# Attended values as plain float32 products of 64 columns, two heads side by side, without a split of the probabilities

## What is computed

```python
q = rms_norm(h @ wq_a, q_a_norm_w) @ wq_b            # 16 heads, 64 latent + 64 rotary columns
compressed_kv, k_pe = split(h @ wkv_a)                # 64 + 64, the same for all heads
attn = einsum('bhqd,bhkd->bhqk', query, key) * SCALE  # 512 x 512 per sequence and head
attn = softmax(attn, axis=-1)
out = einsum('bhqk,bhkd->bhqd', attn, value)          # "attended values"
return out.reshape(b, s, NH * 64) @ wo
```

## Time and profile before

| | |
|---|---|
| median of 3 runs | 1203.41 us (1202.18 to 1204.48) |
| profiled execution: its own time | 1212.62 us |
| its span, first to last instruction | 1210.8 us |
| mean granted TensorE clock | 0.956 |
| busy share of the span | PE 86%, weight loads 72%, DVE 68%, ACT 51%, POOL 41% |
| instructions | PE 6200, DVE 1750, ACT 1340, POOL 464 |

### The profile page before, as it was taken

The page is one execution under the profiler, slowest core; times in us unless marked ns, Lnnn a source line. Parts: engine busy times, 40 slices in busy tenths (PEclk is TensorE's granted clock), DMA queues, the critical chain, the costliest instruction groups (busy, mean ns, idle before and its releaser), DMA issues.

```text
span 1210.8 us, 24733 instructions
## 1 busy us (share of the span) xinstructions
PE 1046.0 (86%) x6200; PEld 865.9 (72%) x6201; DVE 822.8 (68%) x1750; ACT 617.0 (51%) x1340; POOL 501.7 (41%) x464
## 2 busy tenths in 40 slices
PE   4559999997446999999999999999989739999995
PEld 4537777786434788888888888888778627777784
DVE  6354665544674999999999999999834455566542
ACT  2232433422113888888888888888810123343321
POOL 2532233233233455555555555555412532233332
PEclk9999999999676999999999999999999859999998
DMA  9733544422200011111111000101464464454230
GB/s 241 244 128 67 138 100 100 104 47 27 70 0 1 10 36 36 35 35 35 35 35 34 27 31 31 35 35 35 140 217 144 131 209 96 106 141 102 48 54 11
DMA packets 71562, 95.41 MB, mean 79 GB/s; under 512 B 9600, under 2 KB 48640, under 8 KB 71296
## 3 DMA queue, kind: packets, MB, share of 16 engines
q1 hardware_dynamic: 57216, 78.04, 20.8%
q0 software_dynamic: 14304, 16.87, 7.9%
HBM read 64.37 MB, written 34.43 MB: 82 GB/s over the span
## 4 chain that ended last, share of the span: by engine, by line
PE 73%; issue 10%; DVE 6%; POOL 3%; ACT 3%; DMA 1%; another core or an unknown queue 1%; DVEq 1%; ACTq 0%; SPq 0%; POOLq 0%
PE bank L1537 9%; PE bank L1553 7%; PE bank L1356 6%; PE bank L1354 5%; PE bank L1527 5%; PE bank L1358 5%; PE bank L1554 5%; PE bank L1528 5%; PE bank L1529 5%; PE bank L1339 3%; PE bank L1366 3%; PE bank L1368 3%; PE bank L1367 3%; PE bank L1516 2%; PE bank L1517 2%
## 5 line engine op out<-in xcount | busy, mean ns | idle before, releaser
L811 ACT ACTIVATE shared<-bank,small 128x512 f32<-128x512 f32 x256 | 176.1, 688 | 58.6 <-DVE small L1186 56.3
L1186 DVE TENSOR_REDUCE small<-bank 128x1 f32<-128x512 f32 x256 | 175.3, 685 | 38.8 <-PE bank L1529 28.5
L1216 DVE TENSOR_TENSOR split_rows_and_inner<-bank,shared_split 128x512 fp32r<-128x512 f32 x256 | 174.7, 683 | 7.3 <-ACT shared_split L820 5.9
L762 ACT CAST split_rows_and_inner<-bank 128x512 fp32r<-128x512 f32 x78 | 45.9, 588 | 257.0 <-PE bank L1339 232.0
L1537 PE MATMUL bank<-constants,shared 128*128 128x128 f32 x1024 | 155.7, 274 | 0.9 <-ACT shared L811 0.9
L1553 PE MATMUL bank<-shared_split 128*128 128x256 f32 x512 | 144.1, 304 | 5.5 <-DVE shared L1210 2.3
L820 ACT CAST shared_split<-bank 128x512 fp32r<-128x512 f32 x256 | 147.6, 577 | 1.0 <-PE bank L1537 1.0
L1356 PE MATMUL bank<-expert_weights_low,split_rows_and_inner 128*128 x312 | 144.0, 462 | 0.0
L1358 PE MATMUL bank<-expert_weights_high,split_rows_and_inner 128*128 x312 | 143.0, 458 | 0.0
L1553 PEld LDWEIGHTS bank<-shared_split 128*128 128x128 f32 x512 | 96.2, 188 | 56.8 <-issue 27.9
L1554 PE MATMUL bank<-split_rows_and_inner,shared_split 128*128 128x256 f32 x512 | 132.7, 282 | 0.0
(11 more groups left out here) (191 smaller groups left out, 2480.6 us busy)
## 6 DMA issues: line engine op xcount, KB each, us to landing
expert_weights<-L_ffn_w_kernel SPq DMA_DIRECT2D x32, 512.0 KB
shared<-rows_by_expert SPq DMA_DIRECT2D x78, 129.0 KB, 2.4
expert_weights<-L_ffn_wo_kernel SPq DMA_DIRECT2D x16, 512.0 KB
shared<-inverse_sums SPq DMA_DIRECT2D x64, 128.0 KB, 2.8
attended_transposed<-shared SPq DMA_DIRECT2D x32, 256.0 KB, 2.8
expert_weights<-attended_transposed SPq DMA_DIRECT2D x2, 2048.0 KB, 10.1
shared<-attended_transposed SPq DMA_DIRECT2D x2, 2048.0 KB
rows_by_expert<-empty_rows SPq DMA_DIRECT2D x23, 129.0 KB
```

The lines of the kernel that those rows point to most:

```text
L811: nc.scalar.activation(prob[k % 2], bank[k % 4][:, :], ACT.Exp, bias=negmax[:, k % 8:k % 8 + 1], accum_out=psum[par][:, k % 8:k % 8 + 1]). ...
L1186: V.tensor_reduce(negmax[:, k % 8:k % 8 + 1], bank[k % 4][:, :], AX.X, ALU.max, negate=True).then_inc(max_ready, 1)
L1216: V.tensor_tensor(pTl[k // 2 % 2][:, :, at], bank[4 + k % 2][:, :].rearrange("p (c n) -> p c n", c=GT), pTh[k // 2 % 2][:, :, at].bitcast( ...
```

## The change

The two heads of a pair are worked on in turn: tile k is head k % 2, queries k // 2. The transposed probabilities are copied once, as plain float32, tiles 0, 1, 4, 7 by ACT and 2, 3, 5, 6 by DVE, into four buffers (half, head). `attend` takes one chunk c of one half for both heads: two float32 products with 64 columns of values, one into partitions 0 to 63 of bank 6, one into 64 to 127. A half has 256 queries of both heads and eight such products; half 0 is computed at k = 5, 6 and 7 (two chunks at 7), half 1 at k = 0 to 3 of the next pair; k = 4 has none. The lower parts of probabilities and values, `add_lower` and ACT's `take_output` are gone. DVE takes the whole of bank 6 out once a pair, at k = 4. The split query weights have two buffers, and their second fill no longer waits for a query product. The diff, cut (left out: unchanged lines around the edits, names of semaphores, the query products' buffer index, waits in SP's list, the setup's value copies, the removed `add_lower` and ACT's `take_output`):

```diff
@@ -52,8 +52,10 @@
-F32_SHARED = 13 * S + P
-F32R_SHARED = 4 * GT * 3 * HD + 8 * S + 2 * GT * 2 * P + 2 * 3 * P
+F32_SHARED = 11 * S + P
+PT_WORDS = 2 * 2 * GT * 2 * P
+F32R_SHARED = 8 * S + PT_WORDS + (B + 2) * GT * HD + 4 * 3 * P
+BY_ACT, BY_DVE = (0, 1, 4, 7), (2, 3, 5, 6)
...
@@ -266,19 +267,19 @@
-        raw, rawl, inv, att = ([area((5 + 2 * n + k) * S, [S]) for k in range(2)] for n in range(4))
-        invT = area(13 * S, [P], 8)
+        raw, inv, att = ([area((5 + 2 * n + k) * S, [S]) for k in range(2)] for n in range(3))
+        invT = area(11 * S, [P], 8)
         o = 0
         qh, ql = ([[split_area(split, o + (4 * k + 2 * par + hh) * S, [S]) for hh in range(2)] for par in range(2)]
                   for k in range(2))
         o += 8 * S
-        pTh = [split_area(split, o + k * GT * 2 * P, [GT, 2 * P]) for k in range(2)]
-        pTl = [split_area(parts, k * GT * 2 * P, [GT, 2 * P]) for k in range(2)]
-        o += 2 * GT * 2 * P
-        vcur = [split_area(split, o + par * 2 * GT * 3 * HD, [2, GT, 3 * HD]) for par in range(2)]
-        o += 4 * GT * 3 * HD
-        wch, wcl = (split_area(split, o + k * 3 * P, [3, P]) for k in range(2))
+        pT = [[area(F32_SHARED + o + (half * 2 + hh) * GT * 2 * P, [GT, 2 * P]) for hh in range(2)] for half in range(2)]
+        o += PT_WORDS
+        values = area(F32_SHARED + o, [B, GT, HD])
+        o += B * GT * HD
+        vcur = [area(F32_SHARED + o + par * GT * HD, [GT, HD]) for par in range(2)]
+        o += 2 * GT * HD
+        wch, wcl = ([split_area(split, o + (2 * k + par) * 3 * P, [3, P]) for par in range(2)] for k in range(2))
...
@@ -360,6 +360,17 @@
+        def tile(k):
+            return k % 2, k // 2
+        def wait_pT(eng, p, k):
+            if k in BY_ACT:
+                eng.wait_ge(pT_by_act, p * len(BY_ACT) + BY_ACT.index(k) + 1)
+            else:
+                eng.wait_ge(pT_by_dve, p * len(BY_DVE) + BY_DVE.index(k) + 1)
...
@@ -558,25 +569,22 @@
-            def load_weights(p, used):
+            def load_weights(p, par, used):
                 a = p % PAIRS if isinstance(p, int) else pool.snap(p % PAIRS)
                 src = wpair[:, bass.ds(a, 1), :, :].rearrange("p a s n -> p (a s) n")
                 if used is not None:
                     pool.wait_ge(qz_psum, used)
-                nc.gpsimd.tensor_copy(wch, src).then_inc(wc_high, 1)
+                nc.gpsimd.tensor_copy(wch[par], src).then_inc(wc_high, 1)
                 pool.wait_ge(wc_high, p + 1)
                 pool.sem_inc(wc_low_due, 1)
-                nc.gpsimd.tensor_tensor(wcl, src, wch.bitcast(F32), ALU.subtract).then_inc(wcur_ready, 1)
+                nc.gpsimd.tensor_tensor(wcl[par], src, wch[par].bitcast(F32), ALU.subtract).then_inc(wcur_ready, 1)
             def load_values(p, par, used):
                 if used is not None:
                     pool.wait_ge(o_psum, used)
-                high, low = (src[:, bass.ds(p // PAIRS, 1), :, :] for src in (vh, vl))
-                nc.gpsimd.tensor_copy(vcur[par][:, :, :, HD:2 * HD], high.to_broadcast([P, 2, GT, HD]))
-                nc.gpsimd.tensor_copy(vcur[par][:, 0, :, :].rearrange("p t (n c) -> p t n c", n=3)[:, :, 0:3:2, :],
-                                      low.rearrange("p a t n -> p t a n").to_broadcast([P, GT, 2, HD])).then_inc(vcur_ready, 1)
+                nc.gpsimd.tensor_copy(vcur[par].unsqueeze(1), values[:, bass.ds(p // PAIRS, 1), :, :]).then_inc(vcur_ready, 1)
...
@@ -649,13 +643,10 @@
-                    load_weights(p + 2, p + 2)
+                    load_weights(p + 2, par, p + 1)
                 if not last:
                     rope_lower(p + 1, 1 - par)
-                if not among(p, 0):
-                    add_lower(p - 1, 1 - par)
-                if not last:
-                    load_values(p + 1, 1 - par, None if among(p, 0) else p * 4)
+                    load_values(p + 1, 1 - par, None if among(p, 0) else p * 2)
...
@@ -805,20 +795,23 @@
+                hh, qt = tile(k % 8)
                 act.wait_ge(max_ready, s + 1)
                 if not first:
                     act.wait_ge(pT_psum, s - 1)
                 nc.scalar.activation(prob[k % 2], bank[k % 4][:, :], ACT.Exp,
                                      bias=negmax[:, k % 8:k % 8 + 1],
-                                     accum_out=psum[par][:, k % 8:k % 8 + 1]).then_inc(exp_ready, 1)
-            def high_probs(p, k, first):
+                                     accum_out=psum[par][:, hh * GT + qt:hh * GT + qt + 1]).then_inc(exp_ready, 1)
+            def copy_pT(p, k, first):
+                hh, qt = tile(k)
+                half = qt // 2
                 act.wait_ge(pT_psum, p * 8 + k + 1)
-                if k % 2 == 0 and not (first and k < 4):
-                    act.wait_ge(o_psum, p * 4 + k // 2 - 1)
-                nc.scalar.copy(pTh[k // 2 % 2][:, :, (k % 2) * P:(k % 2 + 1) * P],
-                               bank[4 + k % 2][:, :].rearrange("p (c n) -> p c n", c=GT)).then_inc(pT_high, 1)
+                if k in (BY_ACT[0], BY_ACT[2]) and not first:
+                    act.wait_ge(o_psum, p * 2 + half - 1)
+                nc.scalar.copy(pT[half][hh][:, :, (qt % 2) * P:(qt % 2 + 1) * P],
+                               bank[4 + k % 2][:, :].rearrange("p (c n) -> p c n", c=GT)).then_inc(pT_by_act, 1)
...
@@ -847,13 +832,10 @@
-                    if k == 2 and not first:
-                        take_output(p - 1, 1 - par, 1)
-                    if k == 6:
-                        take_output(p, par, 0)
                     if not (last and k == 7):
                         exp(s + 1, k + 1, par if k < 7 else 1 - par, first and k < 1)
-                    high_probs(p, k, first)
+                    if k in BY_ACT:
+                        copy_pT(p, k, first)
...
@@ -1201,20 +1182,22 @@
-            def take_output(p, par, hh):
-                rows_, low_rows = slice(hh * HD, (hh + 1) * HD), slice((1 - hh) * HD, (2 - hh) * HD)
-                dve.wait_ge(o_psum, p * 4 + hh * 2 + 2)
-                if hh == 0 and not among(p, 0, 1):
+            def take_output(p, par):
+                dve.wait_ge(o_psum, p * 2 + 2)
+                if not among(p, 0, 1):
                     dve.wait_ge(att_ready, p - 1)
-                V.tensor_copy(rawl[par][rows_], bank[6][low_rows, :]).then_inc(rawl_sb, 1)
-            def low_probs(p, k):
-                dve.wait_ge(pT_high, p * 8 + k + 1)
-                at = slice((k % 2) * P, (k % 2 + 1) * P)
-                V.tensor_tensor(pTl[k // 2 % 2][:, :, at], bank[4 + k % 2][:, :].rearrange("p (c n) -> p c n", c=GT),
-                                pTh[k // 2 % 2][:, :, at].bitcast(F32), ALU.subtract).then_inc(pT_low, 1)
+                V.tensor_copy(raw[par], bank[6][:, :]).then_inc(raw_sb, 1)
+            def copy_pT(p, k, first):
+                hh, qt = tile(k)
+                half = qt // 2
+                dve.wait_ge(pT_psum, p * 8 + k + 1)
+                if k in (BY_DVE[0], BY_DVE[2]) and not first:
+                    dve.wait_ge(o_psum, p * 2 + half - 1)
+                V.tensor_copy(pT[half][hh][:, :, (qt % 2) * P:(qt % 2 + 1) * P],
+                              bank[4 + k % 2][:, :].rearrange("p (c n) -> p c n", c=GT)).then_inc(pT_by_dve, 1)
...
@@ -1223,10 +1206,8 @@
-                    if k == 2 and not first:
-                        take_output(p - 1, 1 - par, 1)
-                    if k == 6:
-                        take_output(p, par, 0)
+                    if k == 4 and not first:
+                        take_output(p - 1, 1 - par)
...
@@ -1237,20 +1218,21 @@
-                    low_probs(p, k)
+                    if k in BY_DVE:
+                        copy_pT(p, k, first)
                     if k in (3, 4) and first:
                         latent_lower(p + 1, 1 - par, k - 3)
             ropes(0, 0)
             ropes(0, 1)
-            dve.wait_ge(v_split, B * 2 + 1)
+            dve.wait_ge(v_kept, B)
             latent_lower(0, 0, 0)
             latent_lower(0, 0, 1)
             row_max(0, 0)
             row_max(1, 1)
             head_pairs(dve, pair)
             invert_sums(NPAIR - 1, 1)
-            take_output(NPAIR - 1, 1, 1)
+            take_output(NPAIR - 1, 1)
...
@@ -1531,28 +1513,28 @@
-                if not (first and k < 2):
-                    pe.wait_ge(pT_low, s - 1)
+                if k > 1:
+                    wait_pT(pe, p, k - 2)
+                elif not first:
+                    wait_pT(pe, p - 1, k + 6)
                 for c in range(GT):
                     last = tr(bank[4 + k % 2][:, c * P:(c + 1) * P], prob[k % 2][:, c * P:(c + 1) * P], ident)
                 last.then_inc(pT_psum, 1)
-            def attend(p, par, half, piece, first=False):
-                hh, at = half // 2, slice((half % 2) * 2 * P, (half % 2 + 1) * 2 * P)
-                if piece == 0:
+            def attend(p, par, half, c, first=False):
```

(44 more changed lines are left out.)

56 lines of the change are left out of this document (16 added, 40 removed).

## The result

| | before | after |
|---|---|---|
| median | 1203.07 us (4 runs, 1202.18 to 1204.48) | 1237.38 us (4 runs, 1236.89 to 1238.28) |
| ratio | | 1.0285 [1.0267, 1.0303]: slower |
| profiled execution | 1212.62 us | 1237.51 us |

The change made the kernel 34.3 us slower. The two profiled executions differ by only 24.9 us, since the one of before spent some 8.5 us more in its first stage: in its first mixture L1366 first starts at 101.4 us, and L1348, its counterpart in after, at 92.8. So the comparison goes loop by loop, not span by span. From the first to the last scores of attention it was 494.6 us before (380.97 to 875.52) and is 532.5 after (368.85 to 901.36): 38.0 us longer. The setup between the first projection and the first scores is 3.6 us shorter (67.52, now 63.89), and what lies between the last scores and the output product 0.5 us shorter (6.95, now 6.42).

What follows compares the result with a forecast made beforehand. PE was taken to bound the attention loop: 13.9 to 14.0 us of work plus 1.05 of waits gave 15.05 against 15.5 a pair, 14.4 us gained, with 1.8 from setup 16: median 1187 us, range 1165 to 1266.

Steps and rivals of the forecast that it cites:

- rival A: Attention loop: the forecast itself, median 1187 us, own range 1176 to 1200 by DVE's run; chance 0.50.
- rival B: Ends of each attended group cost, by non-overlapping slots (0.21 us) or form changes (0.13 to 0.26); 1231 us, chance 0.20.
- Step (2): Array form changes around attended groups, seven a head pair: taken as nothing, upper end 1.8 us a pair.
- Step (1): Attended products: 32 single-pass ones, 3.8 us a head pair, replaced by 16 float32 ones taken at 3.4 us.
- Rival C: Attended products: no overlap with 128 rows, 3.4 us more a pair, 17.5 in all, 1265 us; chance 0.17.
- step (4): DVE's run ahead of tile 6: PE waits 0.8 to 1.5 us once a head pair, 0.9 taken.
- rival E: Attention loop: clock low throughout, 14 us a pair becomes 28, some 400 us slower; chance 0.05.
- Step (3): Transposed probabilities: fewer DVE and ACT instructions; the whole 1.2 us of PE waits a pair taken as gone.
- Step (5): POOL before the attention loop: query weights split earlier, without waiting for a query product; 1.8 us gained.
- Step (6): After the last head pair: four chunks left, 1.7 us against 0.94, waits shrink; zero, give or take 1 us.
- Rival D: Tile 6: PE doesn't wait for DVE; 14.2 us a pair, 43 us faster, 1160 us; chance 0.08.

Runs made afterwards that it cites:

- Experiment 1: Changed kernel plus a block of single products of several forms between full ones: float32 with 64 columns measured +0.144 us going in, +0.20 coming out.
- experiments 1 and 2: The second: changed kernel plus another block, with other products directly behind float32 ones of 64 columns: +0.146 us before single-pass, +0.12 before transpose, +0.20 before full float32.
- experiment 4: Changed kernel with attended products 128 columns of weights wide, one after the other (attended values not computed): ratio to before 1.0582, period 17.87 us.
- experiment 5: Changed kernel with DVE's output copy at k=4 cut to 64 of 512 columns: ratio to before 1.018, period 16.35 us.
- experiment 6: Changed kernel with the second fill of query weights waiting again for a query product: ratio to before 1.0297; first query product to first scores 11.14 us against 9.26.

## Why the prediction was wrong

It forecast 1187 us, faster; it was 1237.4, slower. The forecast's mechanism, rival A, fell at one step, and rival B, which had a chance of 0.20, held with its second cause, the changes of form: 1231 was its price. That this came so near is in part luck, since its 0.26 us a group was read from 64-row transposes in a slow stretch: the view says 1.00 there, but the transposes of L1296 just ahead (27.64 to 29.58 us) stand 0.213 us apart, as they do at the granted clock of 0.50 (961 to 968 us), and 0.109 at 1.00 (940 to 948 us). The stated range, 1165 to 1266, held the result only because it took in the rivals on both sides of no change.

**Step (2), the changes of form, is the one that failed.** It said "the changed product keeps all 128 rows as L1560 does, so I take nothing", with 0.26 us a group as the upper end. It measured 0.29 to 0.35 a group, above that end, 2.1 us a pair, 67 us in all before anything covers it. The evidence was L1560, and L1560 is a transpose. Experiment 1 put a transpose and a plain float32 product with the same 128 rows and 8 columns side by side: the one is free, the other pays 0.10 and 0.20. So between these two the kind of product decides. No row of before could price the change: it has no plain float32 product of fewer than 128 columns next to a full one, since L1463 follows other 64x64 products and a wait comes after it. The one row with a price, L1434, was set aside for its 64 rows; nothing had shown that only rows count. Its 0.26 was taken as "possibly half at the full" clock. No run has these transposes at another speed (sixteen take 1.91 us in every run), but the single-pass product of 64 rows in experiment 1 pays 0.14 and 0.20 at 1.00, which speaks against halving.

That a transpose is no evidence for a product came out only with the runs: transposes with 64 columns among full products pay nothing (experiments 1 and 2), like L1560 with its 8, and plain float32 products of 64 pay. At such a change the next load starts only 0.09 us after the slot of the product ahead is over, and the price is 0.29 to 0.35 us a group.

**Step (1), the products, was right.** Two instructions advance together: 0.43 us a chunk, 3.4 a pair. Rival C (no overlap) is excluded by the twos and by experiment 4. Before the result no run showed its term: L1463 was seen at one speed, 0.427 us between its twos (7.04 us in all, and 7.04 for its counterpart L1445 in every later run). The 0.43 us a chunk, on which the 3.4 of the sum, the 5.3 of step (4) and the 1.7 of the tail rest, was an estimate that took half of that for the full clock. In its place after showed 0.216 us between twos at the granted clock of 1.00. The factor of two stands in other lines of before: L1296 above, and L1304 with 0.213 us from start to start at 0.50 (from 964.11 us) and 0.112 at 1.00 (from 946.14). The 28 us a pair of rival E are the same factor on 14.

**Step (3), the waits of 1.2 us gone:** the lines behind them are gone and DVE and ACT wait for PE; what is left is in step (4). **Step (4), DVE's run:** the place is right, ahead of tile 6, and the mechanism too (experiment 5). The wait is about 0.6 us a pair where 0.9 was taken, as rival B had it, whose switches lengthen PE's own work in that time (the 0.3 less is not split further by any run); in the stretch the profile shows 12.0 us of idle ahead of L1521, 0.46 a pair, the rest is in the distance of the ends.

The sum, with what was measured: transposes 3.5, scores 5.5, queries 1.4, a small transpose 0.1, products 3.4, switches 2.1, the wait 0.6, together 16.6, against 16.8. The 0.2 left is the small waits for which 0.15 was taken.

**Step (5), the setup:** 1.9 us by experiment 6 where 1.8 was taken. The stage gained 3.6 in all: 2.4 between the first query product and the scores (11.65, now 9.26), of which 0.5 is not this wait, and 1.2 ahead of the query product (55.87 us from the projection, 54.63 now). The copies and waits of the values may hold both; that was not tried. **Step (6), the tail:** -0.5, within its bounds. Rival D (no wait at tile 6) is excluded by the profile, rival E by the granted clock of 1.00.

The forecast was also thin: it gained 0.45 us a pair, while the step taken as nothing occurred seven times, so 0.07 us a group would have spent it. The turning point lies between 4 groups a pair (0.9934 of before) and 7 (1.0285), and the runs have both sides of it.

## What to carry to other kernels

Before a product takes another form of the array, count how often a stream goes in and out of that form, and price the way in and out from a row of the same kind of product. Where the trace has no such row, as here, a block of single products like that of experiment 1 gives the price in one run. Then gather such products, as far as the waits allow. Gathering has an optimum, since products taken out of a step leave it thin for the engines beside it: here three groups a pair (15.24 us) beat two (15.74) and four (15.44), with one placement tried of each. Where an estimate gains less per round than an unpriced step could cost, price that step first.

## What the runs showed of the hardware

- Plain float32 products with 64 columns of weights among full ones cost +0.145 us going in, +0.15 (to transposes) or +0.20 us (to 128-column products) coming out, at the granted clock of 1.00, with 64 or 256 moving columns and with 1 to 8 products in a group. With 8 columns it is +0.10 and +0.20.
- Transposes and single-pass (float32r) products with 128 rows and 64 or 8 columns show no cost among full ones. A single-pass product with 64 rows and 64 columns does (+0.14, +0.20).
- At such a change the next weight load starts 0.09 us after the slot of the product ahead is over, where in a stream it starts within 0.02 us of that product, and its own time is then not hidden (0.107 us with 128 columns, 0.055 with 64, 0.007 with 8, 0.058 for transposes).
- Two float32 products of 64 columns in the two halves overlap fully, though each is two instructions: they are recorded 0.007 us apart, in twos 0.21 apart; in one half they run one after the other, 0.216 each.
- A switch shows here in no busy time and no releaser. It shows as a later start of PE and its loads ("issue", 73.3 and 57.0 us in after from 420 to 860 us) and as a longer first instruction (0.430 us for 0.379), so it is read from the distance between ends.
